# Corner table rows interleaved in SBUF and stored whole; the weighted sum reads runs of four

## What is computed

```python
off, mask = om(x1)                      # offsets and softmax weights from x1 = gelu(layernorm(depthwise3x3(x)))
xpad = pad(x @ in_w + in_b, 1 pixel)    # N, 34, 34, C; the border is zero, without the bias
# per pixel, group g (16 of them, 32 channels each) and tap k (9): a position (px, py), and
v00, v01, v10, v11 = xpad at (y0, x0), (y0, x0+1), (y0+1, x0), (y0+1, x0+1), zero outside
samp = (v00*(1-wx) + v01*wx)*(1-wy) + (v10*(1-wx) + v11*wx)*wy
out = sum over k of samp * mask
```

## Time and profile before

| | before |
|---|---|
| median of 3 runs | 13929.05 us (13926.29 to 13938.86) |
| span of the profiled execution | 13924.7 us |
| busy over the span | PE 61%, DVE 70%, ACT 35%, POOL 66% |
| L133 gathers | 9216, mean 1003 ns |
| L170 sums | 1024, mean 2112 ns |
| DMA packets | 905629, of them 697682 under 512 B |

### The profile page before, as it was taken

The page is one execution under the profiler, slowest core; times in us unless marked ns, Lnnn a source line. Parts: engine busy times, 40 slices in busy tenths (PEclk is TensorE's granted clock), DMA queues, the critical chain, the costliest instruction groups (busy, mean ns, idle before and its releaser), DMA issues. The chain is left out here.

```text
span 13924.7 us, 109987 instructions
## 1 busy us (share of the span) xinstructions
PE 8471.0 (61%) x32544; PEld 4119.1 (30%) x32544; DVE 9755.5 (70%) x9864; ACT 4858.7 (35%) x13537; POOL 9244.7 (66%) x9221
## 2 busy tenths in 40 slices
PE   5783667356665558456665558456665558466667
PEld 3241324132332324232332324232332224222223
DVE  6745986569775887669775887669775887644443
ACT  3232533145331543145331543145331543122221
POOL 0005777777777777777777777777777777777771
PEclk7896778667887679767887679767887679787888
DMA  1002121421233112421233112421233112432221
GB/s 71 9 22 65 54 62 53 116 81 53 60 86 109 53 52 60 114 81 53 60 86 109 53 51 60 114 81 53 60 86 109 53 52 60 113 122 83 93 82 49
DMA packets 905629, 1001.99 MB, mean 72 GB/s; under 512 B 697682, under 2 KB 707922, under 8 KB 893075
## 3 DMA queue, kind: packets, MB, share of 16 engines
q0 software_dynamic: 294912, 604.57, 15.6%
q1 hardware_dynamic: 610066, 389.88, 9.1%
HBM read 814.38 MB, written 179.39 MB: 71 GB/s over the span
## 5 line engine op out<-in xcount | busy, mean ns | idle before, releaser
L133 POOL DMA_INDIRECT gat<-corner_tables,idx x9216 | 9244.3, 1003 | 4377.0 <-issue 2737.3
L170 DVE TENSOR_REDUCE dcn<-gat 128x32 f32<-128x1152 f32 x1024 | 2162.3, 2112 | 297.5 <-ACT gat L150 264.1
L150 ACT ACTIVATE gat<-gat,wts 128x32 f32<-128x32 f32 x8752 | 1906.2, 306 | 727.6 <-DMA gat<-corner_tables,idx 727.1
L797 PE MATMUL PS<-hc,ident 128*128 128x512 f32 (+2 forms) x4096 | 1961.6, 639 | 236.4 <-DVE hc L841 194.0
L164 DVE TENSOR_TENSOR gat<-gat,wts 128x1152 f32<-128x1152 f32 (+3 forms) x1024 | 1094.7, 1069 | 1071.1 <-DMA gat<-corner_tables,idx 960.8
L864 DVE TENSOR_TENSOR_SCAN hs<-dA,PS 128x1024 f32<-128x1024 f32 x672 | 1531.8, 2279 | 45.5 <-ACT dA L814 18.1
L797 PEld LDWEIGHTS PS<-hc,ident 128*128 128x128 f32 x4096 | 1016.0, 281 | 859.1 <-issue 477.2
L1152 ACT ACTIVATE E<-PS,nmax 128x1024 f32<-128x1024 f32 x512 | 570.5, 1114 | 878.3 <-DVE nmax L1209 729.9
L1073 PE MATMUL PS<-ident,E 128*128 128x128 f32 x4096 | 591.4, 291 | 358.6 <-ACT ET L1142 204.7
L841 DVE TENSOR_TENSOR hc<-hs,PS 128x1024 f32<-128x1024 f32 x672 | 802.1, 1194 | 0.8 <-issue 0.8
L1742 PE MATMUL PS<-late_M,wp 128*32 128x512 f32 x4480 | 619.2, 702 | 256.3 <-DVE wp L1783 172.4
(11 more groups left out here) (251 smaller groups left out, 11005.6 us busy)
## 6 DMA issues: line engine op xcount, KB each, us to landing
gat<-corner_tables,idx POOLq DMA_INDIRECT x9216
corner_tables<-xp SPq DMA_DIRECT2D x1024, 64.0 KB, 2.2
D<-in_dist_dram SPq DMA_DIRECT2D x8, 4096.0 KB, 14.5
keep_scratch<-X SPq DMA_DIRECT2D x15, 2048.0 KB, 11.2
weighted<-M SPq DMA_DIRECT2D x56, 512.0 KB, 2.8
late_M<-weighted SPq DMA_DIRECT2D x7, 4096.0 KB
wqkv<-in_qkv_w_dram SPq DMA_DIRECT2D x8, 3072.0 KB, 11.5
X<-keep_scratch SPq DMA_DIRECT2D x12, 2048.0 KB, 16.3
```

What stands on the lines that cost most here:

```text
L133: nc.gpsimd.indirect_dma_start(bd.gat[n % self.NG][:, k * 4 * CG:(k + 1) * 4 * CG], None, bd.rows, bass.IndirectOffsetOnAxis(ap=bd.idx[:, ...
L150: ins = nc.scalar.activation(block, block, ACT.Copy, scale=weights[:, i:i + 1])
L170: nc.vector.tensor_reduce(bd.dcn[m % 2][:, g * CG:(g + 1) * CG], gat[:].rearrange("p (k c) -> p c k", c=CG), AX.X, ALU.add).then_inc(self. ...
L797: mm = nc.tensor.matmul(PS[:, p.ybank(d, h), 0:p.hl], self.ident[:], src[:, j, h * p.hl:(h + 1) * p.hl], start=(c == 0 and j == 0), stop=( ...
```

## The change

- The four corners' rows are projected by themselves. `XN` is now a padded image of 34x34 with zeros around it (`border`, three memsets in norm2), and table position n holds, for corner a, the projection of padded position n + 34 (a // 2) + a % 2. There are 1136 positions, so nine tiles (eight of 128, one of 112), each projected four times: 36 times one bias matmul and four more. The bias row is multiplied by `inside`, which is 1 in the image and 0 on the border.
- ACT copies each projection to `xp` with a step of four elements, so a position's row is channel outside, corner inside. SP stores a tile with one DMA, 8 KB a partition. `xp` has three buffers of 8 KB. One pair of the depthwise sums is copied after 18 of the 36 copies, the other after all.
- The table now writes its border itself, so only the second table is still zeroed.
- The weighted product and the sum see the blocks as [tap, channel, corner]: the sum reads runs of four. ACT's part has a step of four elements, and in power 12 blocks, not 10.
- The depthwise taps read the padded image, so all have 1024 elements. `pos`, `flo` and `tmp` take the room of `XN` and `xp`; DVE waits for the stores before it writes `tmp`.

```diff
@@ Gather.scale
-                block, i = gat[:, k * CG:(k + 1) * CG], n * KP * 4 + k
+                block, i = corners[:, k // 4, :, k % 4], n * KP * 4 + k
@@ Gather.weigh
-        v = gat[:].rearrange("p (k c) -> p k c", c=CG)[:, blocks:, :]
-        wv = bd.wts[:].rearrange("p n (k a) -> p (n k) a", a=1)[:, n * KP * 4 + blocks:(n + 1) * KP * 4, :]\
-            .to_broadcast([P, KP * 4 - blocks, CG])
+        k0 = blocks // 4
+        v = gat[:].rearrange("p (k c a) -> p k c a", c=CG, a=4)[:, k0:]
+        wv = bd.wts[:].rearrange("p n (b a) -> p n b a", b=1)[:, n * KP + k0:(n + 1) * KP]\
+            .to_broadcast([P, KP - k0, CG, 4])
...
-                                gat[:].rearrange("p (k c) -> p c k", c=CG), AX.X, ALU.add).then_inc(self.summed, 1)
+                                gat[:].rearrange("p (k c a) -> p c k a", c=CG, a=4), AX.XY, ALU.add)\
+            .then_inc(self.summed, 1)
@@ group_norm
+                    if padded:
+                        dst = dst[:, 0:PW * PW].rearrange("p (h w) -> p h w", w=PW)[:, 1:H + 1, 1:W + 1]
+                        src = src.rearrange("p (h w) -> p h w", w=W)
@@ l2_prepare_in, SP
-                for m in range(PT):
-                    sp.wait_ge(xp_ready, m + 1)
-                    for yy in range(4):
-                        for corner in range(4):
-                            sp.dma_start(table[y0, x0:x0 + W, :, corner, :],
-                                         xp[m % 4][yy * W:(yy + 1) * W, :].rearrange("p (g c) -> p g c", g=G))\
+                for m, (at, n) in enumerate(tiles):
+                    sp.wait_ge(xp_ready, 4 * (m + 1))
+                    sp.dma_start(table[at:at + n, :], xp[0:n, m % XPB, :]).then_inc(stored[m % XPB], 16)
+                sp.wait_ge(self.second_zero, 16 * 2)
@@ l2_prepare_in, PE
-                for m in range(PT):
-                    if m >= 4:
-                        pe.wait_ge(xp_ready, m - 3)
-                    nc.tensor.matmul(PS[:, m % 4, :], self.ones[0:1, :], self.inb2[:], start=True, stop=False)
+                for i, (m, a, at, n) in enumerate(corners):
+                    if i >= 4:
+                        pe.wait_ge(xp_ready, i - 3)
+                    nc.tensor.matmul(PS[0:n, i % 4, :], self.inside[:, at:at + n], self.inb2[:], start=True, stop=False)
                     for k in range(CT):
-                        mm = nc.tensor.matmul(PS[:, m % 4, :], XN[:, k, m * P:(m + 1) * P],
+                        mm = nc.tensor.matmul(PS[0:n, i % 4, :], XN[:, k, at:at + n],
                                               w_in[:, k, :], start=False, stop=(k == CT - 1))
@@ l2_prepare_in, ACT
+                for i, (m, a, at, n) in enumerate(corners):
+                    if i == len(corners) // 2:
+                        summed(0)
+                    act.wait_ge(xp_done, i + 1)
+                    if m >= XPB and a == 0:
+                        act.wait_ge(stored[m % XPB], 16 * (m // XPB))
+                    nc.scalar.activation(xp[0:n, m % XPB, :].rearrange("p (f a) -> p f a", a=4)[:, :, a],
+                                         PS[0:n, i % 4, :], ACT.Copy).then_inc(xp_ready, 1)
+                summed(2)
@@ l2_prepare_in, DVE
+                for i in range(XPB):
+                    dve.wait_ge(stored[i], 16 * slots[i])
@@ l3_power
-            self.background(block, self.share["power"], ticks=ITERS, blocks=10, first=prefetch if late else None,
+            self.background(block, self.share["power"], ticks=ITERS, blocks=12, first=prefetch if late else None,
```

More of the change, by code:

```diff
@@ L36 @@
 PW = W + 2
+TPOS = H * PW + PW + 14
+TROWS = TPOS * G
+PADN = 1184
 NOFF, NMSK = G * KP * 2, G * KP
@@ L385, in constants @@
         self.inb2 = self.sb(ctx, "inb2", [1, C])
+        self.inside = self.sb(ctx, "inside", [1, PADN])
         self.omb = self.sb(ctx, "omb", [P, NOFF + NMSK])
@@ L400, in _ @@
                 sp.dma_start(self.omb[:, NOFF:], io["mask_b"][:].to_broadcast([P, NMSK])).then_inc(loaded, 16)
-                sp.wait_ge(made, 1)
             @block.vector
             def _(dve):
-                nc.vector.memset(self.gat[0][:], 0.0).then_inc(made, 1)
+                nc.vector.memset(self.inside[:], 0.0).then_inc(made, 1)
+                nc.vector.memset(self.gat[0][:], 0.0).then_inc(vorder, 1)
                 nc.vector.memset(self.slot[:], 0.0).then_inc(vorder, 1)
@@ L413, in _ @@
                 nc.vector.tensor_copy(self.pick[:], self.sel[:]).then_inc(vorder, 1)
-                dve.wait_ge(vorder, 7)
+                dve.wait_ge(made, 1)
+                nc.vector.memset(self.inside[:, 0:PW * PW].rearrange("p (h w) -> p h w", w=PW)[:, 1:H + 1, 1:W + 1], 1.0)\
+                    .then_inc(vorder, 1)
+                dve.wait_ge(vorder, 9)
             @block.scalar
@@ L429, in _, with group_norm @@
                 pool.wait_ge(a_signed, 1)
-    def group_norm(self, ctx, tag, XN, sync=None, first=None):
+    def group_norm(self, ctx, tag, XN, sync=None, first=None, padded=False):
         nc, X, PS = self.nc, self.X, self.PS
@@ L1271, in l2_prepare_in @@
         w_om = self.sb(ctx, "w_om", [P, CT, NOFF + NMSK])
-        xp = [self.sb(ctx, f"xp{i}", [P, C]) for i in range(4)]
+        xp = self.sb(ctx, "xp", [P, XPB, 4 * C])
         x1 = self.sb(ctx, "x1", [P, CT, N])
@@ L1285, in load, with border @@
             sp.dma_start(io["keep"][bass.ds(b, 1)].rearrange("a p t f -> p (a t) f"), X[:]).then_inc(x_kept, 16)
-        self.group_norm(ctx, "2", XN, sync=load)
+        def border(dve):
+            nc.vector.memset(XN[:, :, 0:PW + 1], 0.0).then_inc(bordered, 1)
+            nc.vector.memset(XN[:, :, 2 * PW - 1:(H + 2) * PW - 1].rearrange("p t (h w) -> p t h w", w=PW)[:, :, :, 0:2],
+                             0.0).then_inc(bordered, 1)
+            nc.vector.memset(XN[:, :, (H + 1) * PW + 1:PADN], 0.0).then_inc(bordered, 1)
+            dve.wait_ge(bordered, 3)
+        bordered = self.sem("bordered")
+        self.group_norm(ctx, "2", XN, sync=load, first=border, padded=True)
         names = ("xp_done xp_ready dw_sum dw_ready mean2_done cent2 sq2_ready var2_done sd2_ready norm2 gelu_out "
@@ L1358, in _, with summed @@
             def _(act):
[L1359 to L1367, removed]
+                def summed(pair):
+                    for t in (pair, pair + 1):
+                        act.wait_ge(dw_sum, t + 1)
+                        nc.scalar.activation(x1[:, t, :].rearrange("p (a f) -> p a f", a=2),
+                                             PS[:, 4 + 2 * (t % 2):6 + 2 * (t % 2), :], ACT.Copy).then_inc(dw_ready, 1)
+                for i, (m, a, at, n) in enumerate(corners):
[7 more added lines that the diff above has]
+                summed(2)
                 for t in range(CT):
@@ L1396, in _ @@
                         for t in (pair, pair + 1):
[L1397 to L1401, removed]
+                            out = PS[:, 4 + 2 * (t % 2):6 + 2 * (t % 2), :].rearrange("p a (h w) -> p (a h) w", w=W)
+                            win = XN[:, t, 0:PW * PW].rearrange("p (h w) -> p h w", w=PW)[
+                                :, 1 + dy:1 + dy + H, 1 + dx:1 + dx + W]
                             wk = self.col("dw_w", t * KP + 3 * (dy + 1) + dx + 1)
@@ L1847 @@
 SLOTS = 2
+XPB = 3
 def image(bd, b, share):
```

52 lines of the change are left out of this document (25 added, 27 removed).

## The result

The changed kernel takes 14386.1 us (median of four runs, 14380.9 to 14387.1), the kernel before in the same job 13928.7: 457 us more, ratio 1.0328 (1.0313 to 1.0343). The forecast was 14230 in a range of 14090 to 14350, so the sign was right, and the size lies 36 us above the range. The profiled execution's span is 14384.9 us.

The account below looks back on a forecast made before the run. It took DVE to bound the scan, PE attention, a chain of waits prepare, with POOL second nearly everywhere; six images (+186), image 1 (+20) and image 0 (+95) made +301 on 13924.7, median 14230 us, range 14090 to 14350.

Parts of the forecast that it names:

- the cap: Front of an image: POOL's 1.302 us a gather limits the cheaper sum's saving to -42 us an image, not -55.
- the tail of prepare: Prepare after the mean: waits for gathers go (-8.8 us) and cheaper sums save about 3, taken together as -12.
- image 1: Image 1 as a whole: +41 us, less some 21 in a front that POOL nearly holds, so +20.
- The projections (PE): Prepare: 36 projections in place of 8 keep PE busy 171.1 us and put the mean off by 82.8 us.
- the two waits for gathers go, -8.8: Tail of prepare: POOL fills all five buffers while DVE waits for PE, so both waits vanish, -8.8 us.
- that wait hides under PE now: Image 1's prepare: the extra 32 us from 19 units waiting for POOL hides behind PE's projections, -32 us.
- -55 an image on the path, uncapped: All stages with units: of -768 ns a unit for the sum, -55 us an image lies on the path without POOL's limit.
- The power stages (0): Seven power stages: POOL holds them and 12 blocks on ACT balance the cheaper sum, 0, at most 15 us either way.
- The saving counts in full: Rival, 8%: POOL's pace is no floor, all 768 ns of 112 units count, -86 us an image, total 13817 us.
- POOL gives way in part: Rival, 17%: in the images the full -55 us and a little more is saved, total 14120 to 14160 us.
- The sum gets no cheaper: Rival, 7%: three dimensions or runs of four cost the sum what the step did, total 14503 us.
- ACT's step is dear: Rival, 3%: past 524 ns a block ACT bounds the scan; at 600, +70 us an image, about 14700 us.

Follow-up runs that it names:

- e3: The changed kernel with one projection a tile in place of four, all four corners holding the same values: 13696.2 us, ratio 0.9836.
- e4: The changed kernel with eight gathers a unit in place of nine, the ninth tap's rows never fetched: 13793.2 us, ratio 0.9904.
- e5: The kernel before with eight gathers a unit in place of nine, the ninth tap's rows never fetched: 13562.0 us, ratio 0.9742.
- e6: The changed kernel with six units moved from attention to prepare in images 2 to 7, seven in image 1: 14240.3 us, ratio 1.0225.
- e1: The kernel before with only the new order of product, ACT's blocks and sum, 12 blocks in power, old table: 13752.8 us, ratio 0.9876.

## Why the prediction was wrong, and where it was right

The way was right and the dear part, the projections, within 1 us. The time came out 36 us above the range because three terms for what POOL lets through were too favourable: the cap (-42 an image, measured -28), the tail of prepare (-12, measured -5) and image 1 (+20, measured +75).

- **The projections (PE): right.** 171.1 us of PE were forecast, the mean at 182.1 us came at 181.4, and image 0, with nothing beside it, gave +96.8 for +95. e3 takes three quarters of the projections out and with them 690 us. PE's pace stayed 4.69 us a projection, as its timeline shows from the second on (9045.58, 9050.27). The terms listed for the mean make 8930.7 us and not 8931.3; the 0.6 us that ends image 0's sum is in it unsaid.
- **The stores: right.** Nine issues, landing in 3.9 to 5.3 us, never on the path. e3 shows what they and ACT's copies leave: the mean 32 us earlier than before.
- **The tail: the step "the two waits for gathers go, -8.8" failed.** POOL does fill its buffers while DVE waits for PE, but then stops: in this prepare it waits 79.2 us for DVE's sums. Five buffers hold five units (a buffer comes free with the sum of the unit five back), the tail consumes ten, and the other five units' 45 gathers are issued inside the tail. The waits went from 8.8 to 7.0 us; the tail gave 5 us, not 12.
- **Image 1: the step "that wait hides under PE now" (-32) failed for the same reason.** It has 19 units, 13 of them in the tail, and there DVE waited six times for gathers, 36.0 us before and 35.8 after. POOL stands 77.1 us waiting for DVE, nearly all of it while DVE waits for PE. A wait hides only up to the buffers between the two engines. This is 32 of the 55 us missed there. Its front gave back 1.7 us in place of 21, attention alone going from 386.8 to 404.7 us: POOL held it whole.
- **Norm2 (+2): nothing.** 14.5 us became 14.7 from barrier to barrier: the memsets take about what the cheaper sum of its one unit gives.
- **The sum: right.** -768 ns were forecast, -759 measured, and the scan fell to 499.1 (forecast 500 to 510).
- **ACT's step of four: right in kind.** 339 ns for 306, so +33 where +24 was worked out. The Trainium skill's page "SBUF — State Buffer" (section "Door 1: The DMA port swizzle") lets fp32 step by up to four elements for free; neither this nor the copy of 512 elements at 1.07 us for 0.60 agrees, and the measurement decides.
- **-55 an image on the path, uncapped: right.** e4 against e5 gives 60.5.
- **"-42, capped by POOL": the cap was counted too loosely; it is -28.** Its price was right: from 7703.3 us to the end of unit 111's last gather (9006.7) 995 gathers take 1303.4 us, and without the 7.9 us of waits for sums and grants that is 1.302 us a gather, as forecast. Its count was not. I set the 1008 gathers that DVE needs by the end of norm2, and 6 us, against that end. But DVE's last wait for one, for unit 111, ends inside attention at 9008.2, and the front goes on for 30.0 us behind it, 15 of attention and 15 of norm2, which POOL can't shorten. An estimate from the forecast's own rows: from 7388.3 us on, 996 gathers at 1.302 us, 7.9 us of waits, 1.5 from the last gather to its product and these 30.0 make 1336 us in place of 1361, a gain of 25; the front of this image gained 26, the six on average 28. (The gather at 7388.3 us is the image's fourth and not its first, which starts at 7378.9; the 1008 should have been 1005, which would have made the forecast still more favourable.) e6, which moves units behind this point, and e4, which lowers the floor, both get more out of the same sum.
- **The power stages (0): right,** as POOL held them; e4 and e5 lower them by 150 and 154 us.

Of the rivals none took place. *The saving counts in full* falls by e1: 86 us in each of seven images and 89 in the power stages would be -691, and it gave -171. *POOL gives way in part* would have been faster than the forecast, and POOL gave way less. *The sum gets no cheaper* and *ACT's step is dear* fall by their groups. The range was too narrow on its upper side: three estimates of what POOL would let through (the cap, the tail, image 1) rest on one picture of its lead, and failed together in one direction.

## What to carry to other kernels

When an engine is second in line all over, count its work up to the last point at which someone waits for it, not up to the end of the stretch; a saving elsewhere is capped there. A wait for a producer hides under another engine's idle time only as far as the buffers between them reach, so consumers have to stand in that idle time themselves; six units an image moved there, and seven in image 1, were worth 146 us here. And where a layout makes one access cheap, price what builds it in the engine's own time first: projecting each position four times cost 690 us for a sum that gave 171.

## What the runs showed of the hardware

- A step of four fp32 elements costs on ACT too: 0.92 ns an element out of PSUM (0.60 to 1.07 us for 512), and 33 ns on a block of 32.
- A sum whose innermost run is four adjacent elements, the nine runs 512 bytes apart, costs what a sum of adjacent elements does: 1353 ns against the 1344 of L1442 in the earlier trace rows.
- POOL's gathers slow beside some DVE instructions. In the tail of prepare, while DVE runs element-wise operations and casts with all operands in SBUF, single gathers take 2.5 to 3.0 us, not 0.94, as POOL's and DVE's timelines show for the same microseconds:

```profile
9275.43 2.86 POOL L136 DMA_INDIRECT gat<-corner_tables,idx  x1 [0.30 <-issue]
9278.59 2.49 POOL L136 DMA_INDIRECT gat<-corner_tables,idx  x1 [0.31 <-issue]
9281.38 2.99 POOL L136 DMA_INDIRECT gat<-corner_tables,idx  x1 [0.30 <-issue]
```

```profile
9274.22 2.55 DVE L1471 TENSOR_TENSOR XN<-om,basepos 128x2304 f32<-128x2304 f32 x1
9276.81 1.36 DVE L1472 TENSOR_SCALAR XN<-XN 128x2304 f32<-128x2304 f32 x1
9278.20 1.36 DVE L1473 CAST ints<-XN 128x2304 int32<-128x2304 f32 x1
9279.60 1.36 DVE L1474 CAST XN<-ints 128x2304 f32<-128x2304 int32 x1
9281.00 2.56 DVE L1478 TENSOR_TENSOR om<-XN 128x2304 f32<-128x2304 f32 x1
```

Over the whole execution of the kernel before, 524 of the 9216 gathers take over 1.3 us, and each of the 524 runs beside such an instruction, most often a product (L164). Of the 3850 gathers whose only company of 0.5 us or more is an instruction with an operand in PSUM, none takes that long, and none of the 1089 that have only a reduction (mostly L170) beside them. So the strided sum, which the first rival names, was not what slowed them; the changed kernel has 554 of them. The queue's own load doesn't explain them either: with eight gathers a unit (e5) the tail of prepare has 46 gathers in place of 53, and 15 slow ones as before. No run here takes those DVE instructions away, so this is shown by coincidence in time alone. It would be a second reason for the waits that stayed in the tail.
